# Adding expert outputs to their rows by indirect DMA in each step, in place of a gather at the end

## The reference, cut to what matters

```python
x = x + tanh(g_xattn) * _L0_xattn_ref(layernorm(x), ctx, mask, ...)
...
# gated expert layer on y = layernorm(x), T = 8 * 512 tokens
h = rms_weight * (y * rsqrt(mean(y * y) + EPS))
scores = softmax(h @ gate_w.T)
top_w, top_i = top_k(scores, 2)
top_w = top_w / sum(top_w)                      # the two shares
a = einsum('th,eih->eti', h, w1)
g = einsum('th,eih->eti', h, w3)
eo = einsum('eti,ehi->eth', silu(a) * g, w2)    # expert outputs
out = y + einsum('eth,te->th', eo, cw)          # cw: shares at the chosen experts
result = x + tanh(g_ffn) * out
```

## Time and profile before

| | us |
|---|---|
| median of 3 runs (lowest, highest) | 2351.25 (2348.14, 2354.03) |
| the profiled execution | 2337.9 |
| its span, first to last instruction | 2336.1 |
| PE busy | 1937.9 (83%) |
| DVE busy | 1580.0 (68%) |
| ACT busy | 1009.1 (43%) |
| GpSimd busy | 982.3 (42%) |
| mean DMA rate | 114 GB/s |

### The profile page before, as it was taken

How to read it: one execution, slowest core, us unless ns; L and a number is a source line. 1 busy time by engine, 2 the same in 40 slices (tenths; PEclk the granted TensorE clock), 3 DMA queues, 4 the chain that set the end, 5 groups by cost and what they waited for, 6 DMA issues and landing times. The chain is left out here.

```text
span 2336.1 us, 36411 instructions
## 1 busy us (share of the span) xinstructions
PE 1937.9 (83%) x11846; PEld 1441.2 (62%) x11846; DVE 1580.0 (68%) x3025; ACT 1009.1 (43%) x1924; POOL 982.3 (42%) x884
## 2 busy tenths in 40 slices
PE   1797999999999999889378787239999999999930
PEld 0443554545555455444167676239999999999930
DVE  5475777787878877667148888556766767676623
ACT  0164666666666666556243333013333333333310
POOL 6443355555464544432324454403333323233356
PEclk9698999999999999999689898569999999999975
DMA  2655554555545555551112121154545444444336
GB/s 79 130 89 113 114 116 104 113 102 105 119 94 121 108 106 116 97 105 25 64 46 73 46 90 37 72 200 145 162 153 168 147 158 159 144 159 152 114 111 190
DMA packets 121073, 265.38 MB, mean 114 GB/s; under 512 B 15578, under 2 KB 53210, under 8 KB 120564
## 3 DMA queue, kind: packets, MB, share of 16 engines
q1 hardware_dynamic: 102804, 235.27, 39.7%
q0 software_dynamic: 6144, 16.79, 2.2%
q10 hardware_dynamic: 12000, 11.80, 1.4%
HBM read 185.90 MB, written 77.89 MB: 113 GB/s over the span
## 5 line engine op out<-in xcount | busy, mean ns | idle before, releaser
L700 DVE TENSOR_REDUCE nraw<-ps 128x1 f32<-128x512 f32 x1024 | 649.1, 681 | 244.6 <-PE ps L847 243.1
L613 ACT ACTIVATE spare<-ps 128x512 f32<-128x512 f32 x1024 | 571.0, 602 | 377.5 <-PE ps L857 375.9
L1685 POOL TENSOR_TENSOR u_lo<-u_f,u_hi 128x384 fp32r<-128x384 f32 x210 | 214.0, 1019 | 501.6 <-ACT u_hi L1700 501.6
L847 PE MATMUL ps<-kst,qst 50*128 50x512 f32 x1024 | 287.0, 453 | 27.2 <-DVE nraw L700 17.2
L1721 ACT ACTIVATE silu<-ps_e 128x384 f32<-128x384 f32 x210 | 103.5, 493 | 439.4 <-PE ps_e L1759 439.4
L1759 PE MATMUL ps_e<-x_hi,we_hi 128*128 128x384 f32 x840 | 288.5, 343 | 5.0 <-DVE we_lo L1645 5.0
L857 PEld LDWEIGHTS ps<-qst,kst 52*128 52x128 f32 x1024 | 104.6, 187 | 291.1 <-ACT spare L613 202.3
L1759 PE MATMUL ps_e<-x_hi,we_lo 128*128 128x384 f32 x840 | 282.9, 337 | 0.0
L857 PE MATMUL ps<-qst,kst 52*128 52x512 f32 x1024 | 276.4, 506 | 7.8 <-ACT spare L613 7.5
L1759 PE MATMUL ps_e<-x_lo,we_hi 128*128 128x384 f32 x840 | 282.6, 336 | 0.0
L869 PE MATMUL ps<-spare,vaug 128*32 128x512 f32 x2048 | 279.6, 619 | 0.0
(11 more groups left out here) (227 smaller groups left out, 3705.1 us busy)
## 6 DMA issues: line engine op xcount, KB each, us to landing
we_raw<-in_experts_w SPq DMA_DIRECT2D x90, 896.0 KB, 4.7
parts_kept<-parts SPq DMA_DIRECT2D x64, 512.0 KB, 3.4
kst<-parts_kept SPq DMA_DIRECT2D x192, 128.0 KB, 4.8
qst<-parts_kept SPq DMA_DIRECT2D x192, 128.0 KB, 7.1
x_raw<-xs SPq DMA_DIRECT2D x30, 384.0 KB, 3.8
eo<-eo_sb ACTq DMA_DIRECT2D x30, 384.0 KB, 5.5
x<-sum_tok SPq DMA_DIRECT2D x16, 512.0 KB, 2.6
x_tok<-x SPq DMA_DIRECT2D x16, 512.0 KB, 3.8
```

What stands on the lines that cost most here:

```text
L613: act.activation(probs[:, e % 8], ps[:, score_bank(e, par)], ACT.Exp, scale=SCALE).then_inc(exp_made, 1)
L700: dve.tensor_reduce(nraw[:, g % 2, qt, half, i:i + 1], ps[:, max_bank(m, par)], AX.X, ALU.max, negate=True).then_inc(max_made, 1)
L847: pe.matmul(ps[:, max_bank(m, par)], queries[:, qt], kst[block, par, pair, :], start=True, stop=True).then_inc(max_mm, 1)
L1685: pool.tensor_tensor(u_lo[:, it], u_f[:, slot], u_hi[:, it].bitcast(F32), ALU.subtract).then_inc(ulo_made, 1)
```

## The change

The rows in `xs` become 258 wide: behind the 256 features stand the share of the row (with tanh(g_ffn) in it) and the number of its token. In the router stage GpSimd computes the shares of a batch from the gap of the two best logits (`shares`: two powers, two scalings, a copy and an index row); between the first and the second four scatters it waits for the first four to land and overwrites the shares. SP stores the residual rows straight to the output tensor. The loop over periods 3 to 6 is written out. In the expert stage the cleared rows carry token numbers of spare rows behind the output, so that rows that belong to nobody are added there, and two more areas are cleared. There are 29 steps, all written out. In each step GpSimd keeps the shares and targets of the loaded rows; ACT's copy is split in three and applies the share; and GpSimd adds each third to the output rows by an indirect DMA with addition, one after the other (`add`), behind u_lo 4 to 6 of the following step. The next copy waits for the third. The combining stage is gone, as are the tables that only it used.

```diff
-STEPS += STEPS % 2
+DX = D + 2
+SHARE, ROW = D, D + 1
...
# gelu_phase
-        with eng.Fori(1, B // 2 - 1) as j:
-            for k in (1, 0):
-                period(j * 2 + (2 - k), k, True, True, True, True)
+        for i in range(3, B - 1):
+            period(i, i % 2, True, True, True, True)
...
-                    sp.dma_start(scratch["res"][i - 1], x_tok[:, 1 - k]).then_inc(stored, 16)
+                    sp.dma_start(scratch["out"][(i - 1) * S:i * S, :].rearrange("(p q) d -> p q d", q=QT),
+                                 x_tok[:, 1 - k]).then_inc(stored, 16)
...
+            def shares(b, k):
+                pool.wait_ge(picks_made, b + 1)
+                done = b * 5
+                pool.tensor_tensor(share[:, 0], e_col[:, :], gap[:, :], ALU.pow).then_inc(share_step, 1)
+                pool.wait_ge(share_step, done + 1)
+                pool.tensor_scalar(share[:, 1], share[:, 0], 1.0, None, ALU.add) \
+                    .then_inc(share_step, 1)
+                pool.wait_ge(share_step, done + 2)
+                pool.tensor_tensor(share[:, 2], share[:, 1], neg_one[:, :], ALU.pow) \
+                    .then_inc(share_step, 1)
+                pool.wait_ge(share_step, done + 3)
+                pool.tensor_scalar(share[:, 3], share[:, 2], tanh_g[:, 1:2], None, ALU.mult) \
+                    .then_inc(share_step, 1)
+                pool.wait_ge(share_step, done + 4)
+                pool.tensor_copy(hn_tok[:, k, :, SHARE], share[:, 3]).then_inc(share_step, 1)
+                pool.iota(hn_tok[:, k, :, ROW], pattern=[[1, QT]], base=b * S, channel_multiplier=QT,
+                          allow_small_or_imprecise_dtypes=True).then_inc(row_made, 1)
             def scatter(b, k, s):
+                pool.wait_ge(row_made, b + 1)
+                if s == 0:
+                    pool.wait_ge(share_step, b * 5 + 5)
+                else:
+                    pool.wait_ge(scattered, 16 * (2 * QT * b + QT))
+                    pool.tensor_tensor(hn_tok[:, k, :, SHARE], share[:, 3], share[:, 0], ALU.mult) \
+                        .then_inc(turned_made, 1)
+                    pool.wait_ge(turned_made, b + 1)
                 for n in range(QT * s, QT * s + QT):
                     pool.indirect_dma_start(
...
                         if s == 6:
+                            shares(i - 2, k)
                             pool.wait_ge(slots_made, i - 1)
...
-                link(dve.tensor_copy(slots[:, bass.ds(b * 2 * QT, 2 * QT)], slot_f[:, :]))
...
# expert_phase
+            sp.dma_start(scratch["xs"][NE * CAP:NE * CAP + GR, :]
+                         .rearrange("(t p) d -> p t d", p=P), zeros[:, :, :]).then_inc(padded, 16)
+            sp.dma_start(scratch["out"][T:T + GR, :].rearrange("(t p) d -> p t d", p=P),
+                         zeros[:, :, 0:D]).then_inc(padded, 16)
...
-        for k in range(2):
-            body(0, k, False)
-        with eng.Fori(1, STEPS // 2 - 1) as i:
-            for k in range(2):
-                body(i, k, False)
-        for k in range(2):
-            body(STEPS // 2 - 1, k, k == 1)
+        for n in range(STEPS):
+            body(n // 2, n % 2, n == STEPS - 1)
...
+            def keep_rows(i, n, k):
+                pool.wait_ge(x_in[k], i * 16 + 16)
+                if n >= 3:
+                    pool.wait_ge(eo_made, GT * (n - 2))
+                    pool.wait_ge(added, 16 * GT * (n - 2))
+                pool.tensor_copy(shares[:, n % 3], x_raw[:, k, :, SHARE]).then_inc(share_kept, 1)
+                pool.tensor_copy(targets[:, n % 3], x_raw[:, k, :, ROW]).then_inc(target_kept, 1)
+
+            def add(n, t):
+                pool.wait_ge(eo_made, GT * n + t + 1)
+                pool.wait_ge(target_kept, n + 1)
+                if n or t:
+                    pool.wait_ge(added, 16 * (GT * n + t))
+                pool.indirect_dma_start(
+                    out=scratch["out"], in_=eo[:, t], in_offset=None,
+                    out_offset=bass.IndirectOffsetOnAxis(ap=targets[:, n % 3, t:t + 1], axis=0),
+                    compute_op=ALU.add).then_inc(added, 16)
...
                                        ALU.subtract).then_inc(ulo_made, 1)
+                    if it == 0:
+                        keep_rows(i, n, k)
+                    if n and it >= KI - GT:
+                        add(n - 1, it - KI + GT)
             over_steps(pool, body)
+            for t in range(GT):
+                add(STEPS - 1, t)
+            pool.wait_ge(added, 16 * GT * STEPS)
...
             def put_out(n):
                 act.wait_ge(down_kt, n * KI + KI)
-                if positive(n * 16):
-                    act.wait_ge(eo_out, n * 16)
-                act.activation(eo[:, :, :], ps[:, 4:4 + GT, 0:D], ACT.Copy).then_inc(eo_made, 1)
-                act.wait_ge(eo_made, n + 1)
-                act.dma_start(scratch["eo"][bass.ds(n * GR, GR), :].rearrange("(t p) d -> p t d", p=P),
-                              eo[:, :, :]).then_inc(eo_out, 16)
+                act.wait_ge(share_kept, n + 1)
+                if n:
+                    act.wait_ge(added, 16 * GT * n)
+                for t in range(GT):
+                    act.activation(eo[:, t], ps[:, 4 + t, 0:D], ACT.Identity,
+                                   scale=shares[:, n % 3, t:t + 1]).then_inc(eo_made, 1)
```

More of the change, by code:

```diff
@@ L2 @@
 from concourse import mybir
+import math
 from contextlib import ExitStack
@@ L62 @@
 POOL_LO, DVE_LO = (2, 3, 4, 5), (0, 1, 6, 7)
-ROUTE_STEPS = 24
+ROUTE_STEPS = 23
+DX = D + 2
+SHARE, ROW = D, D + 1
 def kind_of(name):
@@ L996, in gelu_phase @@
     h_tok = sb("gh_tok", [P, QT, D])
-    hn_tok = sb("hn_tok", [P, 2, QT, D])
+    hn_tok = sb("hn_tok", [P, 2, QT, DX])
+    gap = sb("gap", [P, QT])
+    share = sb("share", [P, 4, QT])
+    e_col = sb("e_col", [P, QT])
+    neg_one = sb("neg_one", [P, QT])
     a_hi = sb("g_hi", [P, 2, KD, S], F32R)
@@ L1117, in scatter @@
                         .then_inc(scattered, 16)
+            pool.memset(e_col[:, :], math.e).then_inc(consts_made, 1)
+            pool.memset(neg_one[:, :], -1.0).then_inc(consts_made, 1)
+            pool.wait_ge(consts_made, 2)
             residual(0, 0)
@@ L1241, in route_to_picks @@
                 settle()
-                link(dve.tensor_copy(topv[:, bass.ds(b * QT, QT), :], max8[:, :, 0:2]))
+                if b:
+                    dve.wait_ge(share_step, b * 5 - 4)
+                link(dve.tensor_tensor(gap[:, :], max8[:, :, 1], max8[:, :, 0], ALU.subtract))
                 link(dve.tensor_copy(chosen_f[:, :, :], idx8[:, :, 0:2]))
@@ L1489, in expert_phase @@
             nc.sbuf_tensor("past", [P, NE, STEPS], F32) as past, \
-            nc.sbuf_tensor("above", [P, 2 * B * QT, NE], F32) as above, \
-            nc.sbuf_tensor("shift", [P, NE], F32) as shift, \
-            nc.sbuf_tensor("moved", [P, 2 * B * QT], F32) as moved, \
+            nc.sbuf_tensor("trash", [P, GT], F32) as trash, \
             nc.sbuf_tensor("found", [P, 6, STEPS], F32) as found, \
@@ L1513, in _ @@
             step(dve.tensor_copy(counts_i[:, :], count))
-            dve.memset(zeros[:, :, :], 0.0).then_inc(counts_made, 1)
-            dve.wait_ge(iota_s, 1)
+            step(dve.memset(zeros[:, :, :], 0.0))
+            dve.wait_ge(iota_s, 2)
+            dve.tensor_copy(zeros[:, :, ROW], trash[:, :]).then_inc(counts_made, 1)
             over = past[:, :, 0:T // GR + 1]
@@ L1547, in _ @@
             step(dve.tensor_copy(table[:, 1], row))
[L1548 to L1561, removed]
+            dve.tensor_scalar(table[:, 0], expert, float(NE - 1), None, ALU.min) \
+                .then_inc(table_made, 1)
         @block.sync
@@ L1576, in _ @@
                              .rearrange("o p n -> (o p) n")).then_inc(raw_in[c], 16)
-            sp.wait_ge(padded, 16 * NE)
+            sp.wait_ge(padded, 16 * (NE + 2))
     w_hi = sb("we_hi", [P, 2, 3, KD * I], F32R)
     w_lo = sb("we_lo", [P, 2, 3, KD * I], F32R)
-    x_raw = sb("x_raw", [P, 2, GT, D])
+    x_raw = sb("x_raw", [P, 2, GT, DX])
+    shares = sb("shares", [P, 3, GT])
+    targets = sb("targets", [P, 3, GT], U32)
     x_hi = sb("x_hi", [P, 2, KD, GR], F32R)
@@ L1618, in body @@
                 n = i * 2 + k
-                e = sp.value_load(table[0:1, 0, bass.ds(n, 1)], min_val=0, max_val=NE - 1)
-                r = sp.value_load(table[0:1, 1, bass.ds(n, 1)], min_val=0, max_val=NE * CAP - GR)
-                if positive(n * 2 - 2):
+                e = sp.value_load(table[0:1, 0, n:n + 1], min_val=0, max_val=NE - 1)
+                r = sp.value_load(table[0:1, 1, n:n + 1], min_val=0, max_val=NE * CAP)
+                if n >= 2:
                     sp.wait_ge(xt_mm, n * 2 - 2)
+                    sp.wait_ge(share_kept, n - 1)
+                    sp.wait_ge(target_kept, n - 1)
                 sp.dma_start(x_raw[:, k], scratch["xs"][bass.ds(r, GR), :]
@@ L1897, in build @@
         masks = nc.dram_tensor("masks", [2, B + 1, S], F32).ap()
```

(8 more changed lines are left out.)

90 lines of the change are left out of this document (11 added, 79 removed).

## The result

The changed kernel takes **2419.36 us** (median of 4 runs, 2411.75 to 2423.52); the kernel before took 2352.64 us beside it (4 runs, 2348.14 to 2355.37). The ratio is 1.028, with a 95% interval of 1.0247 to 1.0317: slower, where 2296 us and faster were forecast. The profiled execution took 2423.5 us, with a span of 2421.8.

A forecast was written before the change was run, and what follows sets the result against it. Bounds: PE in the expert stage, GpSimd's gather chain in the last, a GpSimd-DVE ring in the router stage. -90.1 - 22.8 + 0 + 40 + 2.5 + 15 = -55.4, from 2351.25 to about 2296 us; range 2262 to 2340.

The forecast's parts named there:

- Parts 1, 2 and 7: Last stage goes, -90.1 us; 29 expert steps for 30, -22.8; written-out loops, 0.
- Part 3: Expert stage: three serial adds per step take 11.1 us, within the 14.1 before the next output copy is due: 0.
- Part 4: Router stage: extra GpSimd work inside the ring with DVE, about 5.7 us per batch: +40 us, bounds 25 and 50.
- Parts 5 and 6: Table: two more clearings, +2.5 us; new end: last adds, then GpSimd's drain, +15.
- (a): Expert stage: adds outlast their gap and the output copy waits; slower from 5.4 us per add; chance 0.20.
- (b): Router stage pays little, +12 us instead of +40, giving 2268 us; chance 0.12.
- (c): Expert stage: instruction supply of written-out steps stalls PE 2 us each, +58, giving 2354 us; chance 0.06.
- (d): Expert stage: issuing the adds holds PE up 3.75 us per step, 109 in all; no chance of its own.

The follow-up runs named there:

- e7: e2 plus shares computed before the batch's last root and a separate tile for second-choice rows, without the wait between scatters: 2250.32 us, ratio 0.958.
- e4: The kernel before, with 29 steps instead of 30 and its router-stage and step loops written out: 2321.96 us, ratio 0.988.
- e2: The changed kernel without waits between the three adds of a step; only the first waits for the step before: 2307.11 us, ratio 0.980.
- e9: The changed kernel, with DVE splitting only 64 of 1792 weight columns from the third step on (wrong outputs): 2342.67 us, ratio 0.995.
- e3: The changed kernel with the three adds behind u_lo 2, 3 and 4 instead of 4, 5 and 6, still in series: 2441.41 us, ratio 1.036.
- e1: The changed kernel with its adds turned into plain indirect scatters (wrong outputs): 2346.60 us, ratio 0.998.

## Why the prediction was wrong

**The bound before** was read rightly: PE's time per step, the last stage as a chain of gathers, GpSimd between two roots in the router stage. e7 confirms the last: with GpSimd's additions taken out from between the roots, the stage is back at its old length.

**Parts 1, 2 and 7** hold. The last stage is gone, the step is worth 23 us, and written-out code costs nothing (e4).

**Part 3 failed, and decides.** The forecast ("Together 11.1, three below the 14.1: 0") should have been 17.4 and +108 us (772.1, against 664 for 29 steps in e2 and e4). Two things were wrong in it. *The price of one add.* 3.3, 4.5 and 3.3 us became 8.1, 4.9 and 4.4. I built it from an undisturbed scatter at 2.4 us plus a guess for the read. Undisturbed, an add takes 4.6 us from issue to issue, as the last step shows, where nothing runs beside it:

```profile
2403.67 1.54 POOL L1725 DMA_INDIRECT out<-eo_sb,targets  x1 [3.02 <-ACT eo_sb L1765]
2408.23 1.54 POOL L1725 DMA_INDIRECT out<-eo_sb,targets  x1 [3.02 <-DMA out<-eo_sb,targets]
2412.86 1.56 POOL L1725 DMA_INDIRECT out<-eo_sb,targets  x1 [3.08 <-DMA out<-eo_sb,targets]
```

Three of these, 13.7 us, would by the forecast's own measure just have fitted into 14.1; no run shows it. The disturbance of the first, 3.5 us, did the rest, and I gave the disturbed price to the second add. The windows of the earlier trace rows showed the DMA engines empty at 1917.5 to 1920; the issue alone, stretched by DVE's subtraction, lasts longer than that emptiness, so the transfer fell into the loaded stretch. In the changed kernel's step the first issue ends at 2236.15, and the windows there read (the last two columns are DMA share and GB/s):

```profile
2233.00:2235.00 2.00, 2.00 (x14) 2.00 (x13) 1.69 (x1) 0.71 (x2) 2.00 (x1) 1.00 0.00 0
2237.00:2239.00 2.00, 2.00 (x14) 2.00 (x13) 0.00 (x0) 0.48 (x1) 0.20 (x1) 1.00 0.96 373
```

I had seen the stretching in the earlier trace rows and priced it at 1.1 us, outside the sum; it was 1.6. The Trainium skill (SBUF — State Buffer, Who interferes with whom) says that a DVE instruction with two SBUF inputs contends with a GpSimd instruction that reads SBUF, but it infers that such a subtraction leaves the writing of DMA descriptors alone; the traces agree with the first and not with the second (issues of 1.65 us at most in e9, of up to 3.23 beside the subtraction). *What stands behind the waits.* I let GpSimd be free at 1926.9, before u_lo 0 of the next step. With a first add of 8.1 us, u_lo 6 starts 10.64 us behind u_lo 4 instead of 4.73, and DVE and PE behind it. That second ring, u_f to u_lo to u_f, was in the text only as a cover, not as a bound with a price; e3 shows that it costs the time even where the copy has all its room, and in the changed kernel it is 31.3 of PE's idle us, beside 44.4 for the copy.

**Part 4** had the mechanism right and the size low: +48.9 instead of +40, within its bounds. From the second root to the next first root it is 20.4 us, not 13.1, so +7.3 instead of 5.7:

```profile
1427.51 1.40 POOL L1106 TENSOR_TENSOR g_rstd<-g_var_eps,neg_half 128x4 f32<-128x4 f32 x1 [5.38 <-DVE g_var_eps L1372]
1428.89 1.00 POOL L1123 TENSOR_TENSOR share<-e_col,gap 128x4 f32<-128x4 f32 x1
1429.98 0.33 POOL L1125 TENSOR_SCALAR share<-share 128x4 f32<-128x4 f32 x1
1430.40 1.11 POOL L1128 TENSOR_TENSOR share<-share,neg_one 128x4 f32<-128x4 f32 x1
1431.62 1.89 POOL L1131 TENSOR_SCALAR share<-share,tanh_g 128x4 f32<-128x4 f32 x1
...
1442.43 0.20 POOL L1145 TENSOR_TENSOR hn_tok<-share 128x4 f32<-128x4 f32 x1 [2.98 <-DMA xs<-hn_tok,slot_now]
...
1447.90 1.06 POOL L1106 TENSOR_TENSOR g_rstd<-g_var_eps,neg_half 128x4 f32<-128x4 f32 x1
```

The powers cost 2.1 as forecast. The scaling by tanh took 1.89 us instead of 0.19 (in five of the eight batches), and the wait in the middle 2.98 instead of about 1.4 (1.6 to 3.9 over the batches). DVE's wait, 20.8 us in the earlier trace rows, became:

```profile
DVE s_tok L1254 <- POOL g_rstd L1106: 63.7, 7, 11.8
```

That is 42.9 us of the 48.9.

**Parts 5 and 6**: the table +4.7 instead of +2.5, and the end 23.6 us instead of 19, since the last copy starts 4.7 us behind the last product, where 3.3 were forecast, and each of its adds takes 4.6 instead of 3.1; what follows their landing is a little shorter than forecast. **The sum** missed by 123.7 us in the stages of the two profiled executions (123.4 by the medians): 108.0 in Part 3, 8.9 in Part 4, 2.2 in the table and 4.6 in the end.

**The rivals.** (a) came true. Its formula gives the shorter steps: 22.76 + (17.4 - 14.1) = 26.1 us, where 15 of 26 distances between copies are 25.9 to 26.7 us; the other 11 are 27.2 to 28.6, the mean of all 26.8, so the formula leaves out some 0.7 us per step. Its turning point of 5.4 us per add was passed, with 5.8 on the mean. Its place was only half right: moving the adds away from the copy (e3) makes it worse, and the cure (e2) removes the series. It had a chance of 0.20, on an upper bound that counted a doubled gather, but not that the first add could meet two disturbances at once. (b), (c) and (d) fell: the router stage pays in full, e4 runs at full rate, and in e2 the same adds cost PE nothing.

## What to carry to other kernels

An indirect DMA whose landing the issuing engine waits for costs that engine issue and landing together, and everything that stands behind it in its program; price the landing in the worst place of the step, and look whether the wait is needed at all: transfers to distinct rows need none among themselves. Before an operation is put on an engine at half load, look whether it falls inside a loop across engines, and move it to where that engine stands idle. Work put into a gap must fit at its disturbed duration, with a second price for the ready work that it delays.

## What the runs showed of the hardware

- An indirect DMA with addition of 128 rows of 256 floats makes 144 packets, a plain one 48. Undisturbed, its issue takes 1.54 us, against 0.96, and the least landing is 3.5 to 3.7 us, against 2.4 for a plain scatter (e1).
- Beside a DVE subtraction of 128x1792 with both inputs in SBUF the issue takes up to 3.2 us (1.65 at most in e9): it ends 1.42 to 1.52 us behind the subtraction's end in all 53 cases of the changed kernel, a plain scatter's 0.86 to 0.89 us behind it in all 53 of e1. So its price is the rest of the subtraction and not a factor. The small scaling of 128x4 took 1.89 us in the changed kernel and 0.31 in e7.
- A PE wait that the profile calls "issue" can be one for another engine: here PE's product starts 0.1 us behind the end of ScalarE's copy.
- Rows of GpSimd can overlap. u_lo behind an add has a row of 1.57 us instead of 1.01, but it starts 0.52 us before the add's row ends, and ends 1.02 to 1.06 us behind it, as behind a plain scatter (e1): its own work is not longer.
